# An eight-batch MLA transformer layer on one core: the next batch's norm and latents placed inside the heads, its queries, keys and rotation inside the feed-forward

## What is computed

```python
x = x + attn(layernorm(x))        # latent attention, 16 heads
x = x + ffn(layernorm(x))         # gated, 512 -> 1536 -> 512
# attn
q  = rmsnorm(h @ wq_a.T) @ wq_b.T            # 384 latents, heads of 128 + 64 (rotated)
kv = h @ wkv_a.T                             # 128 latents + 64 rotated key columns
out = softmax(q k^T / sqrt(192)) v, then @ wo.T
# ffn
silu((h @ fp8(gate_w)) * gate_scale) * ((h @ fp8(up_w)) * up_scale) @ fp8(down_w) * down_scale
```

## Time and profile before

| | us |
|---|---|
| median of three runs | 2515.75 (2514.68 to 2521.54) |
| profiled execution, its own time | 2519.38 |
| span of its trace | 2517.6 |

### The profile page before, as it was taken

The page is one execution under the profiler, slowest core; times in us unless marked ns, Lnnn a source line. Parts: engine busy times, 40 slices in busy tenths (PEclk is TensorE's granted clock), DMA queues, the critical chain, the costliest instruction groups (busy, mean ns, idle before and its releaser), DMA issues.

```text
span 2517.6 us, 38482 instructions
## 1 busy us (share of the span) xinstructions
PE 2313.3 (92%) x11136; PEld 1055.6 (42%) x11136; DVE 1674.9 (67%) x3489; ACT 1090.0 (43%) x2404; POOL 831.9 (33%) x517
## 2 busy tenths in 40 slices
PE   6887789999999989899899998989999998989978
PEld 4333344343543435344443444434354443534433
DVE  6677774777657775577746777477765677557762
ACT  4466632444325543345333543245432544334532
POOL 0322213443144331534225331344314433153422
PEclk9989999999999999999999999999999999999999
DMA  6255520555115540255304551045511654035530
GB/s 228 59 126 125 113 55 34 97 110 94 22 40 118 103 89 4 68 118 105 64 0 107 101 109 38 33 96 108 96 21 38 119 104 90 4 72 98 108 61 17
DMA packets 631583, 200.93 MB, mean 80 GB/s; under 512 B 613344, under 2 KB 613600, under 8 KB 630496
## 3 DMA queue, kind: packets, MB, share of 16 engines
q1 hardware_dynamic: 631520, 200.25, 38.1%
HBM read 40.78 MB, written 8.39 MB: 20 GB/s over the span
## 4 chain that ended last, share of the span: by engine, by line
PE 49%; issue 27%; DVE 8%; POOL 7%; ACT 6%; DMA 1%; SPq 1%; POOLq 0%; DVEq 0%; ACTq 0%
PE bank L244 6%; PE bank L245 6%; PE bank L246 6%; PE scores L244 4%; PE scores L245 4%; PE scores L498 4%; PE scores L246 4%; PE bank L508 3%; PE bank L509 3%; PE bank L510 3%; POOL arena L1206 3%; ACT arena L772 2%; PE scores L495 2%; ACT arena L774 2%; PE bank L613 2%
## 5 line engine op out<-in xcount | busy, mean ns | idle before, releaser
L1192 POOL TENSOR_TENSOR arena<-arena 128x1024 f16<-128x1024 f32 x256 | 544.6, 2127 | 997.0 <-ACT arena L774 997.0
L772 ACT ACTIVATE arena<-scores,shift 128x512 f32<-128x512 f32 x512 | 357.4, 698 | 613.1 <-DVE shift L1024 613.1
L1041 DVE SCALAR_TENSOR_TENSOR arena<-bank,rden,arena 128x512 f32<-128x512 f32 x512 | 350.9, 744 | 157.0 <-PE bank L246 156.9
L1022 DVE TENSOR_REDUCE mx<-scores 128x1 f32<-128x512 f32 x512 | 353.8, 691 | 31.0 <-PE scores L246 20.4
L774 ACT ACTIVATE arena<-scores,shift 128x512 f16<-128x512 f32 x512 | 358.7, 701 | 0.0
L613 PE MATMUL bank<-arena,WFF 128*128 128x512 f16 x1408 | 316.9, 379 | 0.0
L1206 POOL TENSOR_TENSOR arena<-arena 128x512 f16<-128x512 f32 x96 | 113.9, 1186 | 569.5 <-ACT arena L809 569.5
L244 PE MATMUL bank<-WVO,arena 128*128 (+1 forms) x512 | 201.1, 393 | 77.1 <-DVE arena L865 41.4
L1095 DVE SCALAR_TENSOR_TENSOR arena<-arena,bank 128x512 f32<-128x512 f32 x96 | 66.0, 687 | 256.7 <-ACT arena L805 256.7
L865 DVE SCALAR_TENSOR_TENSOR arena<-bank,arena 128x512 f16<-128x512 f32 (+1 forms) x296 | 197.3, 671 | 52.7 <-ACT arena L765 24.7
L613 PEld LDWEIGHTS bank<-arena,WFF 128*128 (+1 forms) x1408 | 137.4, 98 | 164.2
(11 more groups left out here) (132 smaller groups left out, 3472.5 us busy)
## 6 DMA issues: line engine op xcount, KB each, us to landing
arena<-x SPq DMA_DIRECT2D x15, 1024.0 KB, 5.2
arena<-arena SPq DMA_TRANSPOSE x640, 3.2
arena<-w_ffn SPq DMA_DIRECT2D x24, 384.0 KB, 3.5
out<-arena SPq DMA_DIRECT2D x32, 256.0 KB, 2.0
WFF<-w_o SPq DMA_DIRECT2D x4, 1024.0 KB, 18.3
arena<-w_nope SPq DMA_DIRECT2D x4, 768.0 KB, 14.9
arena<-down_scale SPq DMA_DIRECT2D x8, 256.0 KB, 3.3
WFF<-w_pe SPq DMA_DIRECT2D x1, 1536.0 KB, 11.5
```

The costliest lines, as they stand in the source:

```text
L772: act.activation(P32[:, t, :], SC[:, t, :], ACT.Exp, scale=EXP_SCALE, bias=shift[:, t:t + 1], accum_out=esum[:, par, t:t + 1]).then_inc(s[ ...
L1022: dve.tensor_reduce(mx[:, t:t + 1], SC[:, t, :], AX_X, ALU.max).then_inc(s["mxr"], 1)
L1041: dve.scalar_tensor_tensor(out=XR[:, t, :], in0=OBANK[t][:, :], scalar=rden[:, t:t + 1], in1=XR[:, t, :], op0=ALU.mult, op1=ALU.add).then_ ...
L1192: pool.tensor_tensor(PL[:, par, two, :], P32[:, two, :], PH[:, par, two, :], ALU.subtract).then_inc(s["pl"], 1)
```

## The change

Four things move, and the order on every engine is rewritten for them.

1. **Norm of the next batch.** x of batch b+1 is loaded after head 1 (after head 0 in batch 0). Its statistics and Newton steps become five parts of `next_norm` on DVE, one in each of heads 3 to 7 (2 to 6 in batch 0), between the sums and the context. POOL then norms, copies to f16 and takes the low half, one tile in each of heads 7 to 10 (6 to 9). SP turns the result by four crossbar transposes after heads 11 and 12 (10 and 11), in place of 16 PE transposes.
2. **Its latents** are single steps between other PE work at the end of the heads. `last_values` computes head 15's context in two halves, each waiting for its own half of the transposed probabilities, and `last_of_attention` interleaves the adds with the statistics.
3. **Queries, keys and rotation** go between feed-forward chunks: query transposes at chunks 2 and 3, keys at 4, rotations 0 to 5 at chunks 5 to 10, absorb(0) and absorb(1) before the last two down products, rotations 6 and 7 around scores(0) of the next batch. They take the banks `BO` and `BT`, so gate and up have one bank each, `BQ` and `BC`.
4. **Loads and chunks.** The load of the residual moves from behind the stores to behind head 0 of the next batch. The 24 rounding chunks of batch 0 are spread over heads 2 to 15, and small marker writes go.

```diff
+def rounded_in(c):
+    return 2 + c * (NH - 2) // NC_FF
...
+LATENTS = [("q", 0), ("q", 1), ("k", 0), ("k", 1), ("q", 2), ("k", 2), ("q", 3), ("k", 3)]
+CHUNK_QT, CHUNK_KT, CHUNK_ROT = 2, 4, 5
...
+                for i in range(NH):
+                    if i == 6:
+                        sp.wait_ge(s["qpel"], (b + 1) * N_ROT)
+                    head(i, base, i % 2, ahead=i < NH - 2)
+                    if i == 0 and not first:
+                        sp.wait_ge(s["stored"], b * (16 * NT))
+                        sp.dma_start(XR, xb[bass.ds(b, 1)].rearrange("a p t d -> (a p) t d")).then_inc(s["ld_res"], 16)
+                    if i == 1 - sooner and not last:
+                        next_input(b)
+                    if i in (11 - sooner, 12 - sooner) and not last:
+                        turn_input(b, i - (11 - sooner), stg)
...
-                if not last:
-                    sp.wait_ge(s["stored"], b * (16 * NT) + 16 * NT)
-                    sp.dma_start(XR, xb[bass.ds(b + 1, 1)].rearrange("a p t d -> (a p) t d")).then_inc(s["ld_res"], 16)
...
+                scores(b, final, 0)
+                values(b, final - 1, 1)
+                lat = (b + 1) * (2 * NT)
+                if not last:
+                    pe.wait_ge(s["xt1"], (b + 1) * 64)
+                    pe.wait_ge(s["qal"], base + NH)
+                    latent("q", 0)
+                project_out(b, final - 1, 1)
                 scores(b, final, 1)
                 values(b, final, 0)
                 if not last:
+                    pe.wait_ge(s["lat"], lat + 1)
+                    latent("q", 1)
                 project_out(b, final, 0)
...
+                last_values(b, last)
                 project_out(b, final, 1)
...
+                def gate_up(c):
                     n = b * NF + c
+                    for w, dst, freed in ((WG, BQ, "gt"), (WU, BC, "ft")):
+                        pe.wait_ge(s[freed], n)
...
+                        if CHUNK_ROT <= c < CHUNK_ROT + N_ROT - 2:
+                            rotated_ahead(b + 1, c - CHUNK_ROT)
+                if not last:
+                    pe.wait_ge(s["gt"], (b + 1) * NF)
+                    absorb(0, (b + 1) * NH)
+                down(NF - 2)
+                if not last:
+                    absorb(1, (b + 1) * NH + 1)
+                down(NF - 1)
...
+                else:
+                    act.wait_ge(s["yo"], b * NT)
+                probs(base, 0, True)
...
+                maxima(base)
+                qa_lo(base + 2, 0)
+                if not first:
+                    rot_products(b, N_ROT - 1, RBANK[1])
+                    rot_lo(b, N_ROT - 2)
                 dve.wait_ge(s["ld_res"], base + 16)
...
+                    dve.wait_ge(s["outr"], g * NT + t + 1)
+                    ch.add(dve.bn_stats(bn[:, t, :], XR[:, t, :]))
...
+                pool.tensor_scalar(XN[:, t, :], XN[:, t, :], mv[:, t, 0:1], rs_x[:, t:t + 1], ALU.subtract,
+                                   ALU.mult).then_inc(s["x32"], 1)
...
+                pool.tensor_copy(stg[:, 0, t, :], XN[:, t, :]).then_inc(s["xs"], 1)
...
+                pool.tensor_tensor(stg[:, 1, t, :], XN[:, t, :], stg[:, 0, t, :], ALU.subtract).then_inc(s["xs"], 1)
```

More of the change, by code:

```diff
@@ L350, in batch @@
[L350 to L358 removed]
+                sooner = 1 if first else 0
@@ L657, in batch @@
-                ffn(b, 2 * b + 1 if last else 2 * b + 2, last)
-                if not last:
-                    keys_and_rotated(b + 1, b * NT)
+                    pe.wait_ge(s["f_free"], NC_FF)
+                ffn(b, last)
             pe.wait_ge(s["ld_id"], 16)
-            x_transposes(0)
+            for t in range(NT):
+                x_transposes(0, t, XN)
             pe.wait_ge(s["w_lo"], N_A)
-            latents(0, 0)
+            setup_latents(0)
             pe.wait_ge(s["k_scaled"], 1)
@@ L787, in attention @@
[L787 removed]
+                for c in chunks[1:]:
+                    round_chunk(c)
+            def attention(b, last, first):
                 base = b * NH
[L789 to L798 removed]
@@ L820, in batch @@
[L820 to L833 removed]
+                if first:
+                    qa_hi(base + 1, 1)
+                else:
+                    act.wait_ge(s["yo"], b * NT)
@@ new lines, in attention @@
+                probs(base, 0, True)
+                qa_hi(base + 2, 0)
+                if not first:
+                    rot_hi(b, N_ROT - 2)
+                probs(base + 1, 1, False)
+                if not first:
+                    rot_hi(b, N_ROT - 1)
+                qa_hi(base + 3, 1)
+                if first:
+                    for i in range(2, NH - 2):
+                        head_step(i, base, i % 2, chunks=chunks_of(i))
+                else:
+                    with act.Fori(1, NH // 2 - 1) as pair:
+                        i = pair * 2
+                        head_step(i, base, 0)
+                        head_step(i + 1, base, 1)
@@ new lines, in attention, with last_of_attention @@
+                if not first:
+                    rot_lo(b, N_ROT - 1)
+                start = 2 if first else 3
+                for i in range(2, NH):
+                    part = i - start if 0 <= i - start < 5 and not last else None
+                    head_step(i, b, i % 2, ahead=i < NH - 2, chunks=chunks_of(i) if first else (), part=part)
+            def last_of_attention(b):
+                g, u = b * NH + NH - 1, b + 1
+                sums_of_head(g, 1)
+                for half in range(2):
+                    context(b * N_CT + NH - 1 + half, slice(2 * half * P, 2 * half * P + 2 * P), (BC, BQ)[half])
+                ch = Chain(dve, "ln_chain", u * LN_N)
@@ L1102, in tile_step @@
                                              in1=GT[:, par, :], op0=ALU.mult, op1=ALU.mult).then_inc(s["ft"], 1)
-                for c in range(4):
-                    if c == 0 and not last:
+                for c in range(NF):
+                    tile_step(c)
+                    if last:
+                        continue
+                    n = c - CHUNK_ROT
+                    if c == 0:
                         latents_norm(b + 1)
+                    if c == 1:
+                        q_norm(b + 1)
@@ L1166, in _ @@
             keys_lo(0)
-            q_lo(0)
-            keys_and_rotated(0, with_weights=True)
+            for t in range(NT):
+                q_lo(0, t, bank[t])
+            keys_turned(0)
+            setup_rotated()
             batch(0, False, first=True)
@@ new lines, in attention @@
+            def attention(b, last, first):
+                base = b * NH
+                if not first:
+                    rotate(b, N_ROT - 2)
+                start = 6 if first else 7
+                stg = STG_FIRST if first else STG
+                for i in range(NH):
+                    head(base + i, i % 2)
+                    if i == 0 and not first:
+                        rotate(b, N_ROT - 1)
+                    if 0 <= i - start < NT and not last:
+                        next_norm(b, i - start, stg)
@@ L1230, in _ @@
-            batch(0, False)
+            for n in range(N_ROT):
+                rotate(0, n, True)
+            batch(0, False, first=True)
             with pool.Fori(1, B - 1) as b:
```

905 lines of the change are left out of this document (486 added, 419 removed).

## The result

The changed kernel takes **2475.98 us** (median of 4 runs, 2474.62 to 2477.89) against 2518.64 for the kernel before on the same chip: ratio 0.9832, interval 0.9812 to 0.9851. It is 1.7% faster, by 43 us and not by the 77 forecast, and 2476 lies above the range of 2392 to 2470. The profiled execution spans 2474.0 us against 2517.6.

What follows compares the result with a forecast made beforehand. TensorE was taken as the limit, VectorE and ScalarE in batch 0. Each boundary wins 11.3 - 18.5 + 17.8 = 10.6 us, seven 74; batch 0 adds 1, the last 2: 77 less, 2438 against 2515.75, range 2392 to 2470.

Steps and rivals of the forecast that it cites:

- Heads 2 to 13: Twelve heads of a batch: added norm pieces on VectorE, GpSimd steps and SyncE transposes cost nothing; still 134 us.
- Rival (4): Heads 7 to 12: POOL or SP passes its cover, 48 us over 28 heads, 2486 us; chance 0.06.
- End of the heads, 39.8: Scores of head 14 to the gate products: 51.1 us becomes 39.8, 11.3 less; about 12 won in batch 0.
- Feed-forward, 82: Feed-forward takes in key, rotation and absorb work: 63.5 us becomes 82, 18.5 more, with 1.2 and 0.5 exposed early.
- rival (3): Feed-forward, single gate bank: VectorE late at every gate step, PE stops before each gate; about 2607 us, chance 0.05.
- From the last down product to the third head, 31.5: Stretch across batches: 49.3 us becomes 31.5, 17.8 less, with PE pauses of 2.2 and, from the late residual load, 4.6.
- the clock term: Last down product to third head: 3.4 us lost to half clock around two pauses, bounds 1.7 and 5.1.
- Rival (1): Last down product to third head: late residual load does not bite, 44 us more won, 2394 us; chance 0.2.

Runs made afterwards that it cites:

- the run with all edits: Changed kernel with statistics pieces moved, residual wait later, latents' norm ahead of chunk 0's gate step, own bank for chunk 1's gate: 2382.34 us, ratio 0.946.
- the early norm: Changed kernel with the latents' norm on VectorE ahead of chunk 0's gate step instead of behind it: 2473.42 us, ratio to before 0.9829.
- the run with the probes: Changed kernel with statistics pieces moved to ends of heads 4 to 6, plus three small independent VectorE steps in each of heads 8 to 13: 2449.23 us.
- the run with the later wait: Changed kernel with VectorE's wait for the residual load moved from before head 1's maxima to before head 0's output add: 2446.34 us, ratio 0.9718.

## Why the prediction was wrong

**The step that failed is "Heads 2 to 13", the sentence on VectorE**: five pieces of at most 1.4 us in 1.36 us of idleness "before each context: nothing". I compared a length with a gap and didn't ask who else runs in that gap. Three pieces meet GpSimd's L1372 and last 2.2 to 5.1 us. That is +44.8 us, against the 34 us by which the sum missed (77 forecast, 43 measured). The row that warned was in front of me: the POOL row begins at 903.24 and the context at 904.67 after 1.36 us of idleness, so GpSimd starts just as the gap opens. I also took the contention rule of the Trainium skill (GPSIMD Engine Reference, its table of engine properties) to the rotations of the feed-forward alone, where it cost nothing, and read it as a slowing by half a microsecond from the maxima in the earlier trace rows. The rows show no slowing but a hold until the other's instruction ends: 1.80 to 2.06 us beside one of 2.13, 1.01 us beside one of 1.17 (L1029 beside L1406). So its price goes with what is left of GpSimd's instruction, not with the size of VectorE's.

**Rival (4)** gave 48 us to these heads, nearly the right size, for the wrong reason: the GpSimd steps are 2.07, 0.61 and 1.16 us, 3.84 a tile against my 3.5, within the cover of 6.6, and with these steps in place the heads take 134.64 us in the run with all edits. What I gave 0.06 as GpSimd running late was GpSimd standing in VectorE's way; that the size came near is luck.

**End of the heads, 39.8: right.** 39.9 us in batches 1 to 6, TensorE pausing 0.69 and 1.33 us around the transposes where I had 0.85 and 1.3. For batch 0 I took 12 us and it was 5.7; the stretch takes 47 us, not 40. TensorE pauses 3.4 and 1.2 us there before VectorE's adds (L1206), which stand behind the joining of the chunks moved here, and 3.4 us at half clock follow the first. The heads they left won 3.4 us, for which I had nothing.

**Feed-forward, 82: right.** 82.56 us. The two pauses are 1.06 and 1.22 for 1.2 and 0.5. The second was mis-sized by the same hold: of the latents' twelve steps L1029 took 1.01 us where it takes 0.16, beside GpSimd's L1406. Rotations and splits never made a gate late, so rival (3) had no part in it.

**From the last down product to the third head, 31.5: right in its mechanism, 1 to 3 us too long.** The load went out 14.9 us after the last down product (14.5) and landed at 20.3 (20.1) in the batch shown; VectorE's maxima waited for it; the pause before values was 2.02 (2.2), and the one before the projection 4.4 to 4.6 us behind three batches, as forecast (4.6). The size that was off is the clock term: I added 3.4 us of loss to two full pauses. Behind all batches but one (batch 5) there were only 3.41 us at half clock, 1.7 us of loss, and behind four batches they came ahead of the second pause, which shrank to 2.5 to 3.0 us. Where the clock held until the second pause, as in the row of the early norm (4.36), the stretch measured up to 30.2 us. A slow clock ahead of a wait was covered by it here; I counted wait and clock as if they stood in line.

**Rival (1)** rested on the load's place alone causing the wait. Taking the wait off the maxima shortened the seven stretches by 34 us, against my 44: 4.9 us a boundary where I had 6.3.

The other 4 of the 38 us between 2438 and 2476 are the 3.6 us that I took off to get from the profiled execution of before to the median of its runs. That median is now 2518.64, close to the profiled 2519.38, and the profiled execution of after took 2475.89 against a median of 2475.98: there was nothing to take off.

Two readings in the prediction are off without moving the sum. The four windows of the earlier trace rows add up to 297.9 us, not 298.1. And the 15 us per head that I set against the new transposes don't follow from 10.5 us for one of them: two less the 3.56 us free are 17.4. The 1.4 us are the time of an issue on SyncE's queue (1.28 us in the median for the new ones); they land 3.3 us after it, still far from 10.5.

## What to carry to other kernels

Before VectorE work on SBUF goes into an idle gap, look at GpSimd in the same microseconds. If a large instruction runs there, a step of a kind that is held can cost up to that instruction's whole length, even on four numbers; place such steps where GpSimd idles, or use a kind that isn't held. In the view by source line, the sign is a tiny step whose maximum is far over its minimum, or which takes ten times as long as its neighbours of the same size.

Put a wait directly before the first instruction that reads what is awaited. One line moved behind four maxima, sums and context was worth 30 us here.

Price a chain of pauses from its last one: what is won in front of it, or lost to a slow clock in front of it, may show only when the last wait is gone. Four edits won 63 us one by one and 94 together.

## What was unexpected of the hardware

- A VectorE step on 128x4 fp32 in SBUF takes 0.16 us, and up to 2.12 us if it starts behind a 2.13 us GpSimd tensor_tensor; if it starts 0.02 us ahead, it isn't held (the run with the probes). 128x1 scalings, maxima and statistics from SBUF are not held in the same place; a two-tensor step is, even on 128x1.
- Before the change the hold was visible in the difference of the keys' products, 128x128 (L962 of the kernel before: 0.29 us once, and 1.21 the seven times that a GpSimd step had begun 0.10 us ahead of it), and in L985, whose longest was 1.28 for 0.69.
- After a pause of 2.02 us the clock went to 0.50 for 3.41 us; after one of 2.18 us at the same place of the program it stayed at 1.00, and in the run with the later wait it stayed after 2.15 to 2.19 us behind batches 1 to 3 and fell after 2.24 and 2.19 behind batches 4 and 5. The length of that pause alone doesn't decide it.
